# Order of the work inside the turns of the middle stage of a two-layer graph kernel

## The chip, the cores and the metric

The kernel runs on one core of one Trainium2 chip. The metric is the device time of one execution in microseconds (us). Beside the plain executions there is one profiled execution, and every row below is from its trace. Engines are named as in the profile: PE is TensorE, PEld its weight loads, DVE is VectorE, ACT is ScalarE, POOL is GpSimd, SP is SyncE.

## What is computed

100,000 nodes with 32 features and 50,000 edges, sorted by destination. Two residual layers:

```python
h = relu(layernorm(x))
m = einsum('ek,ei,kio->eo', basis(edge_attr_2), h[src], weight)       # 9 basis functions
x = x + segment_sum(m, dst) / max(degree, 1) + h @ root_w.T + root_b  # layer 1
h = relu(layernorm(x))
g = gat_conv(h)                    # 8 heads, softmax over a node's edges and itself
g = layernorm(g + h) * g1 + be1
g = relu(g @ w1 + b1) @ w2 + b2 + g
x = x + layernorm(g) * g2 + be2    # layer 2
```

For most nodes no edge ends there, and their second layer needs only their own row. They are all computed as if this held. The rows of nodes with edges are computed a second time in edge order and written over the first ones at the end.

## The kernel before

**Tiles.** A tile is 125 partitions by 16 rows of 32 features (125x512). The edges are 25 chunks of such a tile (5 blocks of 5, `NB`, `NJ`), the nodes 50 units. A product of a tile first transposes it (four PE transpositions into a bank of `T`, `transpose`, L490; ACT copies the bank into `xT` or `hT`), then multiplies it into a bank of `C` (`product`, L499). There are two `T` banks and two `C` banks, each used in turn, so the third use of a kind waits until the first one's reader is done (`t_done`, `c_done`).

**Stages.** The first stage (to about 710 us) does layer 1's norm and messages. The middle stage, `b_turn` on four engines (PE L652, ACT L968, DVE L1439, SP L342), does three node steps and four edge steps. A later stage (`d_turn`, then `x_early`) gathers the sources' rows of layer 1 for the attention; the last one scatters the finished rows. POOL issues all indirect DMAs of 125 rows each: 400 gathers by source in the first stage, then 400 gathers by destination and 400 scatters of layer 1's rows in the middle stage (for each chunk: `scatter_x1` of chunk c, L448, then `gather_dst` of chunk c+5, L443), 400 gathers in the stage after (they start when all scatters have landed, L467), and 400 scatters at the end (L478).

**Turns.** A chunk takes two turns of the middle stage, a block ten, and the whole stage 50 and two more. `turn(h)` (L108) says which steps a turn holds:

- the unit's steps, in three turns one after the other: `n1` (transpose the node rows, centre them: `product` with `center`; DVE makes relu rows in `hrow` 1), `n2` (transpose those, product with `base_bd` and a bias; DVE divides by the deviation, `hrow` 2), `n3` (transpose those, ACT applies g1 and be1, four products `hidden` (L529), ACT relu, then `back_product` (L536): a bias, 4 centring and 16 small products into one `C` bank, and `finish_rows` (L1401) on DVE, whose `unit_done` lets SP store the unit).
- the edges' steps: `e1` (transpose the gathered rows, centre) in even turns, `e2` (transpose the relu rows, product with `root_bd`) in odd ones; DVE then adds the carried and scaled message sums, which `aggregate` (L1430) makes ready with five operations, and `x1_ready` (L1466) lets POOL scatter the chunk and PE begin `e3`; `e3` (transpose, centre, relu rows) in the next even turn and `e4` (product with `base_bd` through a `T` bank in `to_T`, L550, and the attention logits through a `C` bank, `logits_dst`, L1411) in the next odd turn.

In a block units start in turns 0, 1, 3, 4, 6, 7 and 9 (L48). So n3 and n2 stand in turns 2, 5, 8, n3 and n1 in 3, 6, 9, n2 and n1 in 0, 4, 7, and all three in turn 1.

Every centring product is followed by the same norm chain: ACT squares the bank (`square`, L917), DVE sums it (`spread`, L1231), ACT takes the root (`root`, L925), DVE inverts it (L1240) and scales the rows (`relu_rows`, L1247, or `rows_over_std`, L1254), which also frees the bank. All engines work through their own list in order, so the order in `b_turn` is written out by hand four times.

Of the kernel before, what the change touches and what calls it, by code (L numbers as in the profile page):

```python
# [52 lines left out]
CREDIT = 4  # L53
# [62 lines left out]
def gnn_program(nc, x, src, dst, edge_attr, w0, root_w, root_b, w_gat, att_src, att_dst, bias_gat,  # L116
# [10 lines left out]
    with ExitStack() as ctx:  # L127
# [357 lines left out]
        def _(pe):  # L485
# [4 lines left out]
            def transpose(rows, then=None):  # L490

                at, bank = tq.next()
                pe.wait_ge(t_done, tq.room)
                for g in range(G):
                    i = nc.tensor.transpose(T[bank][:, g * P:(g + 1) * P], rows[:, g * GF:(g + 1) * GF], ident[0:P, 0:P])  # L495
                    i.then_inc(t_ready, 1) if g == G - 1 else None
                return at
# [31 lines left out]
            def hidden(nT, quarters=range(4)):  # L529

                for t in quarters:
                    at, bank = fq.next()
                    pe.wait_ge(f_done, fq.room)
                    mm(V[4 - fq.depth + bank][:, 0:WT], w1_q[:, t, :], nT, start=True, stop=True).then_inc(f_ready, 1)  # L534

            def back_product(nT):  # L536

                at, bank = cq.next()
                pe.wait_ge(c_done, cq.room)
                mm(C[bank][0:P, :], ones[:, 0:P], bias_row[:, 1, :], start=True, stop=True, skip_group_check=True)  # L540
                for g in range(G):
                    mm(C[bank][0:P, g * GF:(g + 1) * GF], nT[:, g * P:(g + 1) * P], center[:, :], start=False, stop=True, skip_group_check=True)  # L542
                for t in range(4):
                    pe.wait_ge(f_done, fq.at - 3 + t + 1 + CREDIT)
                    for g in range(G):
                        i = mm(C[bank][0:P, (4 * g + t) * F:(4 * g + t + 1) * F], hid[:, t, g * P:(g + 1) * P], w2_c[:, :],  # L546
                               start=False, stop=True, skip_group_check=True)
                i.then_inc(c_ready, 1)
# [103 lines left out]
            def b_turn(b, at):  # L652
                t = {}
                if "n3" in at:
                    pe.wait_ge(c_done, st["n2"] + 1 + CREDIT)
                    t["n3"] = transpose(unit(hrow, 2))
                if "n2" in at:
                    pe.wait_ge(c_done, st["n1"] + 1 + CREDIT)
                    t["n2"] = transpose(unit(hrow, 1))
                if "n3" in at:  # L660
                    pe.wait_ge(t_done, t["n3"] + 1 + CREDIT)
                    hidden(xT[:, 2, :])
                if "e3" in at:
                    j, back = at["e3"]
                    pe.wait_ge(x1_ready, (b - back) * NJ + j + 1)
                    t["e3"] = transpose(unit(rows_out, j))
                if "e4" in at:
                    pe.wait_ge(c_done, st["e3"] + 1 + CREDIT)
                    t["e4"] = transpose(normed(4))
                if "n2" in at:  # L670
                    st["n2"] = product(hT[:, 1, :], base_bd[:, :], bias=0, t_at=t["n2"])
                if "e1" in at:
                    j = at["e1"][0]
                    pe.wait_ge(ring_dma[j], (NB + b + 1) * DMAS)
                    t["e1"] = transpose(unit(ring, j))
                if "e2" in at:
                    pe.wait_ge(c_done, st["e1"] + 1 + CREDIT)
                    t["e2"] = transpose(unit(hrow, 0))
                if "n1" in at:
                    k = at["n1"][0]  # L680
                    pe.wait_ge(unit_in[k], (b + 1) * 16)
                    t["n1"] = transpose(place(k))
                if "e3" in at:
                    st["e3"] = product(hT[:, 2, :], center[:, :], t_at=t["e3"])
                if "e4" in at:
                    to_T(hT[:, 3, :], base_bd[:, :], bias=0, t_at=t["e4"])
                    product(hT[:, 3, :], att_bd[:, :, :].rearrange("f t h -> f (t h)"), n=8 * H)
                if "n3" in at:
                    back_product(xT[:, 2, :])
                if "e1" in at:  # L690
                    st["e1"] = product(xT[:, 0, :], center[:, :], t_at=t["e1"])
                if "e2" in at:
                    product(hT[:, 0, :], root_bd[:, :], plus=ring[0:P + 1, at["e2"][0], :], t_at=t["e2"], frees=ring_used)
                if "n1" in at:
                    st["n1"] = product(xT[:, 1, :], center[:, :], t_at=t["n1"])


            pe.wait_ge(v_done, 12 * NC + CREDIT)
# [207 lines left out]
        def _(act):  # L906
# [5 lines left out]
            def evac(to, rows=128, width=WT, func=ACT.Copy, **kw):  # L912
                at, bank = tq.next()
                act.wait_ge(t_ready, at + 1)
                nc.scalar.activation(to, T[bank][0:rows, 0:width], func, **kw).then_inc(t_done, 1)  # L915
# [52 lines left out]
            def b_turn(b, at):  # L968
                if "n3" in at: affine()
                if "n2" in at: evac(hT[:, 1, :])  # L970
                if "e3" in at: evac(hT[:, 2, :])
                if "e4" in at: evac(hT[:, 3, :])
                if "n3" in at: hidden()
                if "n2" in at: square(2)
                if "e1" in at: evac(xT[:, 0, :])
                if "e2" in at: evac(hT[:, 0, :])
                if "n2" in at: root(2)
                if "n1" in at: evac(xT[:, 1, :])
                if "e3" in at: square(4); root(4)
                if "e4" in at:  # L980
                    j, before = at["e4"]
                    k, saves = j % 2, 3 - j % 2
                    if isinstance(b, int) and b - before == 0:
                        if j > 1: act.wait_ge(base_saved[k], 16 * (j // 2))
                    else:
                        act.wait_ge(base_saved[k], 16 * ((b - before) * saves + j // 2))
                    evac(unit(base_out, k), rows=P, width=W)
                    act.wait_ge(t_done, tq.at + 1 + CREDIT)
                    act.sem_inc(base_ready, 1)
                    cq.next()  # L990
                if "n3" in at: square(3)
                if "e1" in at: square(0)
                if "e2" in at: cq.next()
                if "n3" in at: root(3)
                if "e1" in at: root(0)
                if "n1" in at: square(1); root(1)
            tq.restart(); cq.restart(); fq.restart()
            for h in range(HALVES):
                b_turn(0, turn(h, first=True))
# [139 lines left out]
        def _(dve):  # L1139
# [297 lines left out]
                step(v.tensor_tensor(slots(rows), slots(rows), wide(degree[0:P, here]), ALU.mult))  # L1437

            def b_turn(b, at):  # L1439
                norm = {}  # L1440
                if "n2" in at: norm["n2"] = spread(2)
                if "e3" in at: norm["e3"] = spread(4)
                if "e2" in at: aggregate(b, b * NJ + at["e2"][0])
                if "n2" in at: rows_over_std(2, norm["n2"])
                if "e3" in at:
                    j, back = at["e3"]
                    relu_rows(4, norm["e3"])
                    dve.wait_ge(c_done, cq.at + 1 + CREDIT)
                    v.tensor_scalar(diff[0:P, bass.ds(((b - back) * NJ + j) * W, W)], normed(4), 0.0, None, ALU.max)
                if "e4" in at:  # L1450
                    j, back = at["e4"]
                    logits_dst((b - back) * NJ + j)
                if "n3" in at: norm["n3"] = spread(3)
                if "e1" in at: norm["e1"] = spread(0)
                if "n3" in at:
                    rows = place(at["n3"][0])
                    finish_rows(rows, rows, norm["n3"], unit_done)
                if "e1" in at: relu_rows(0, norm["e1"])
                if "e2" in at:
                    j, c = at["e2"][0], b * NJ + at["e2"][0]  # L1460
                    if not isinstance(b, int) or b > 0:
                        dve.wait_ge(rows_landed[j], b * DMAS)
                        dve.wait_ge(x1_saved[j], 16 * b)
                    _, rows = bank_ready()
                    v.tensor_tensor(unit(rows_out, j), rows, msgs[0:P, bass.ds(c * W, W)], ALU.add).then_inc(c_done, 1)
                    v.tensor_copy(index_out[0:P, j, :], scatter_to[0:P, bass.ds(c * CE, CE)]).then_inc(x1_ready, 1)  # L1466
                if "n1" in at: relu_rows(1, spread(1))
            cq.restart()
            steps.restart()
            for h in range(HALVES):  # L1470
# [312 lines left out]
```

## Time and profile before

| | us |
|---|---|
| median of 3 executions | 3253.76 |
| lowest, highest | 3248.36, 3260.42 |
| the profiled execution, its own time | 3263.96 |
| its span from the first to the last instruction | 3262.2 |
| mean granted TensorE clock, share of full speed | 0.794 |

The profile gives start and length of each instruction, and for an engine's idle time the instruction that ended it. "issue" means that nothing the profile shows was waited for.

### The profile page before, as it was taken

To read this page: it belongs to the slowest core of one execution; us is meant where nothing else is said; L and a number is where in the kernel's file an instruction comes from. 1 tells how busy PE (TensorE), PEld (TensorE's weight loads), DVE (VectorE), ACT (ScalarE), POOL (GpSimd) and SP (SyncE) were. 2 spreads that over 40 slices of the span, in tenths; PEclk is the share of its full clock that TensorE was granted. 3 is DMA by queue.
4 is the path that set the end of the run, shared out by engine and by line. 5 is a ranking of instruction groups with operands and counts; after the bars stand their busy time and mean duration, and the time that the engine had idled before them with its cause. 6 is when DMAs were issued, how large, how long until landed. Compare 5 with 4: busy or idle time off the path is not lost.

```text
span 3262.2 us, 33511 instructions
## 1 busy us (share of the span) xinstructions
PE 2247.2 (69%) x10666; PEld 1570.5 (48%) x10666; DVE 1858.0 (57%) x3253; ACT 839.7 (26%) x1614; POOL 2458.8 (75%) x2011
## 2 busy tenths in 40 slices
PE   2787777747777777777777645747767547888740
PEld 1555555525555655565565534534444334454420
DVE  4889889983433433334334322346767567898720
ACT  1333233213322223223222222322222222222210
POOL 7778777887878878787787488888783075878877
PEclk9989889977888778777777766767888667888775
DMA  2333233221111112212111111111110110111100
GB/s 59 85 72 78 68 76 79 53 57 28 38 37 33 39 39 41 40 32 43 37 36 30 24 13 31 25 18 28 21 24 9 45 16 16 40 28 28 35 10 10
DMA packets 116212, 123.93 MB, mean 38 GB/s; under 512 B 70726, under 2 KB 72747, under 8 KB 116070
## 3 DMA queue, kind: packets, MB, share of 16 engines
q0 software_dynamic: 64000, 30.57, 10.0%
q1 hardware_dynamic: 52070, 91.52, 8.8%
q8 instruction: 82, 1.34, 0.2%
q14 instruction: 60, 0.49, 0.0%
HBM read 59.51 MB, written 64.00 MB: 38 GB/s over the span
## 4 chain that ended last, share of the span: by engine, by line
PE 35%; DVE 23%; POOL 22%; issue 11%; ACT 6%; SPq 2%; DMA 1%; DVEq 0%; ACTq 0%; POOLq 0%
POOL ring L430 15%; PE C L546 7%; PE V L534 7%; POOL out_rows L478 6%; PE C L510 5%; PE T L495 3%; DVE region L1595 3%; PE V L795 3%; DVE var L1235 3%; PE C L540 2%; PE C L542 2%; ACT sq L923 2%; DVE region L1587 2%; DVE region L1338 2%; ACT hid L934 2%
## 5 line engine op out<-in xcount | busy, mean ns | idle before, releaser
L430 POOL DMA_INDIRECT ring<-in_x,index x800 | 979.3, 1224 | 244.4 <-issue 243.2
L478 POOL DMA_INDIRECT out_rows<-ring,index_out x400 | 496.7, 1242 | 278.3 <-DVE ring L1407 158.9
L1235 DVE TENSOR_REDUCE var<-sq 125x16 f32<-125x512 f32 x325 | 220.7, 681 | 791.9 <-ACT sq L923 791.4
L452 POOL DMA_INDIRECT x_table<-region,index_out x400 | 483.3, 1208 | 152.4 <-issue 121.0
L430 POOL DMA_INDIRECT ring<-x_table,index x400 | 496.5, 1241 | 124.5 <-issue 123.9
L534 PE MATMUL V<-xT,w_q 128*128 128x500 f32 x600 | 369.0, 766 | 74.2 <-ACT hid L934 41.0
L923 ACT ACTIVATE sq<-C 125x512 f32<-125x512 f32 x300 | 179.4, 598 | 903.5 <-PE C L546 527.0
L510 PE MATMUL C<-center,xT 128*125 128x128 f32 x1400 | 246.2, 335 | 104.9 <-DVE hrow L1257 70.0
L546 PEld LDWEIGHTS C<-w_c,hid 128*125 128x125 f32 x2400 | 313.5, 215 | 0.0
L546 PE MATMUL C<-w_c,hid 128*125 128x32 f32 x2400 | 312.2, 293 | 0.0
L495 PE MATMUL T<-ident,hrow 125*128 125x125 f32 x1000 | 190.1, 328 | 164.0 <-DVE hrow L1251 139.0
L510 PEld LDWEIGHTS C<-center,xT 128*125 128x125 f32 x1400 | 223.7, 240 | 146.6 <-issue 68.6
L568 PE MATMUL V<-region,hT 128*125 128x384 f32 x600 | 250.6, 532 | 61.2 <-DVE region L1330 61.2
L534 PEld LDWEIGHTS V<-xT,w_q 128*128 128x128 f32 x600 | 144.8, 257 | 259.9 <-issue 135.2
L915 ACT ACTIVATE hT<-T 128x500 f32<-128x500 f32 x250 | 146.8, 589 | 446.3 <-PE T L495 446.0
L495 PEld LDWEIGHTS T<-ident,hrow 125*128 125x128 f32 x1000 | 145.0, 173 | 207.2 <-DVE hrow L1251 119.0
L934 ACT ACTIVATE hid<-V,cols 128x500 f32<-128x500 f32 x300 | 190.5, 680 | 98.6 <-PE V L534 98.4
L1338 DVE TENSOR_REDUCE region<-region 125x128 f32<-125x1152 f32 x100 | 211.8, 2119 | 0.0
L795 PE MATMUL V<-gat_bd,hT 128*125 128x512 f32 x320 | 183.0, 694 | 27.3 <-DVE region L1587 25.2
L1595 DVE TENSOR_REDUCE region<-region 125x128 f32<-125x1024 f32 x100 | 187.9, 1899 | 0.0
L1330 DVE TENSOR_TENSOR region<-V,region 125x384 f32<-125x384 f32 x300 | 157.7, 551 | 46.0 <-PE V L568 40.2
L540 PE MATMUL C<-bias_row,ones 128*125 128x512 f32 x150 | 100.2, 756 | 92.0 <-DVE hrow L1257 91.8
(250 smaller groups left out, 3143.8 us busy)
## 6 DMA issues: line engine op xcount, KB each, us to landing
ring<-in_x,index POOLq DMA_INDIRECT x800, 3.3
nodes<-in_x SPq DMA_DIRECT2D x25, 500.0 KB
x_table<-nodes SPq DMA_DIRECT2D x25, 500.0 KB
x_plain<-nodes SPq DMA_DIRECT2D x25, 500.0 KB
nodes<-x_plain SPq DMA_DIRECT2D x50, 250.0 KB
out_rows<-nodes SPq DMA_DIRECT2D x50, 250.0 KB
x_table<-region,index_out POOLq DMA_INDIRECT x400, 2.6
ring<-x_table,index POOLq DMA_INDIRECT x400, 2.7
```

What stands on the lines that cost most here:

```text
L430: pool.indirect_dma_start(out=ring[0:P, j, s * F:(s + 1) * F], out_offset=None, in_=table, in_offset=bass.IndirectOffsetOnAxis(ap=index[0: ...
L452: pool.indirect_dma_start(out=x1_table[:, :], out_offset=bass.IndirectOffsetOnAxis(ap=index_out[0:P, j, s:s + 1], axis=0), in_=rows_out[0: ...
L478: pool.indirect_dma_start(out=out[:, :], out_offset=bass.IndirectOffsetOnAxis(ap=index_out[0:P, j, s:s + 1], axis=0), in_=ring[0:P, j, s * ...
L495: i = nc.tensor.transpose(T[bank][:, g * P:(g + 1) * P], rows[:, g * GF:(g + 1) * GF], ident[0:P, 0:P])
L510: i = mm(C[bank][0:P, g * n:(g + 1) * n], cols_T[:, g * P:(g + 1) * P], right, start=bias is None and plus is None, stop=True, skip_group_ ...
L534: mm(V[4 - fq.depth + bank][:, 0:WT], w1_q[:, t, :], nT, start=True, stop=True).then_inc(f_ready, 1)
L546: i = mm(C[bank][0:P, (4 * g + t) * F:(4 * g + t + 1) * F], hid[:, t, g * P:(g + 1) * P], w2_c[:, :], start=False, stop=True, skip_group_c ...
L795: mm(banks[bank][0:P, :], hT[:, k, g * P:(g + 1) * P], gat_bd[:, q * 512:(q + 1) * 512], start=True, stop=True).then_inc(v_ready, 1)
L934: nc.scalar.activation(hid[:, t, :], V[4 - fq.depth + bank][:, 0:WT], ACT.Relu, bias=cols[:, 0:1]).then_inc(f_done, 1)
L1235: v.tensor_reduce(unit(var, k), slots(squares(k)), AX.X, ALU.add).then_inc(var_ready, 1)
L1338: v.tensor_reduce(msgs[0:P, bass.ds(cv * W + g * GF, GF)], products[0:P, (g % 2) * KS * GF:(g % 2 + 1) * KS * GF].rearrange("p (k c) -> p ...
L1595: v.tensor_reduce(diff[0:P, c * W + g * GF:c * W + (g + 1) * GF], weighted[0:P, (g % 2) * H * GF:(g % 2 + 1) * H * GF].rearrange("p (h c) ...
```

## The change

On PE, `hidden` is split into quarters 0, 1 and 2, 3; both halves stand behind the transpositions of e3 or e4, the second one behind all transpositions. The product of n1 moves from the end of the turn to ahead of the products of e3 and e4, and `back_product` moves to the end. On ACT the same order is kept: n1's copy ahead of n2's root, the second half of `hidden` behind it, n1's square and root ahead of the edges', n3's square and root last. On DVE n2's rows and n1's rows are finished before `aggregate`, each norm is completed before the next begins, and n3's is last. No instruction is added or taken away, but each engine's list is in another order. SP and POOL keep their lists.

```diff
@@ PE
                 if "n2" in at:
                     pe.wait_ge(c_done, st["n1"] + 1 + CREDIT)
                     t["n2"] = transpose(unit(hrow, 1))
-                if "n3" in at:
-                    pe.wait_ge(t_done, t["n3"] + 1 + CREDIT)
-                    hidden(xT[:, 2, :])
                 if "e3" in at:
...
                     t["e4"] = transpose(normed(4))
+                if "n3" in at:
+                    pe.wait_ge(t_done, t["n3"] + 1 + CREDIT)
+                    hidden(xT[:, 2, :], (0, 1))
                 if "n2" in at:
                     st["n2"] = product(hT[:, 1, :], base_bd[:, :], bias=0, t_at=t["n2"])
...
                     t["n1"] = transpose(place(k))
+                if "n3" in at:
+                    hidden(xT[:, 2, :], (2, 3))
+                if "n1" in at:
+                    st["n1"] = product(xT[:, 1, :], center[:, :], t_at=t["n1"])
                 if "e3" in at:
                     st["e3"] = product(hT[:, 2, :], center[:, :], t_at=t["e3"])
                 if "e4" in at:
                     to_T(hT[:, 3, :], base_bd[:, :], bias=0, t_at=t["e4"])
                     product(hT[:, 3, :], att_bd[:, :, :].rearrange("f t h -> f (t h)"), n=8 * H)
-                if "n3" in at:
-                    back_product(xT[:, 2, :])
                 if "e1" in at:
                     st["e1"] = product(xT[:, 0, :], center[:, :], t_at=t["e1"])
                 if "e2" in at:
                     product(hT[:, 0, :], root_bd[:, :], plus=ring[0:P + 1, at["e2"][0], :], t_at=t["e2"], frees=ring_used)
-                if "n1" in at:
-                    st["n1"] = product(xT[:, 1, :], center[:, :], t_at=t["n1"])
+                if "n3" in at:
+                    back_product(xT[:, 2, :])
@@ ACT
-                if "n3" in at: hidden()
+                if "n3" in at: hidden((0, 1))
                 if "n2" in at: square(2)
                 if "e1" in at: evac(xT[:, 0, :])
                 if "e2" in at: evac(hT[:, 0, :])
+                if "n1" in at: evac(xT[:, 1, :])
                 if "n2" in at: root(2)
-                if "n1" in at: evac(xT[:, 1, :])
+                if "n3" in at: hidden((2, 3))
+                if "n1" in at: square(1); root(1)
                 if "e3" in at: square(4); root(4)
...
-                if "n3" in at: square(3)
-                if "e1" in at: square(0)
+                if "e1" in at: square(0); root(0)
                 if "e2" in at: cq.next()
-                if "n3" in at: root(3)
-                if "e1" in at: root(0)
-                if "n1" in at: square(1); root(1)
+                if "n3" in at: square(3); root(3)
@@ DVE
-                norm = {}
-                if "n2" in at: norm["n2"] = spread(2)
-                if "e3" in at: norm["e3"] = spread(4)
+                if "n2" in at: rows_over_std(2, spread(2))
+                if "n1" in at: relu_rows(1, spread(1))
                 if "e2" in at: aggregate(b, b * NJ + at["e2"][0])
-                if "n2" in at: rows_over_std(2, norm["n2"])
                 if "e3" in at:
                     j, back = at["e3"]
-                    relu_rows(4, norm["e3"])
+                    relu_rows(4, spread(4))
...
-                if "n3" in at: norm["n3"] = spread(3)
-                if "e1" in at: norm["e1"] = spread(0)
-                if "n3" in at:
-                    rows = place(at["n3"][0])
-                    finish_rows(rows, rows, norm["n3"], unit_done)
-                if "e1" in at: relu_rows(0, norm["e1"])
+                if "e1" in at: relu_rows(0, spread(0))
...
-                if "n1" in at: relu_rows(1, spread(1))
+                if "n3" in at:
+                    rows = place(at["n3"][0])
+                    finish_rows(rows, rows, spread(3), unit_done)
```

## Rows read from the trace of the kernel before

**Rows 1.** Waits of POOL from 4 to 1786 us: total us, times, longest.
```profile
POOL ring L430 <- issue: 243.2, 796, 0.7
POOL x_table L452 <- issue: 111.9, 367, 0.4
```
**Rows 2.** Timeline of POOL: start us, length us, instruction, idle before it.
```profile
735.99 1.23 POOL L452 DMA_INDIRECT x_table<-region,index_out  x1 [0.30 <-issue]
784.80 1.23 POOL L452 DMA_INDIRECT x_table<-region,index_out  x1 [0.37 <-issue]
...
1786.80 1.19 POOL L452 DMA_INDIRECT x_table<-region,index_out  x1 [2.07 <-DVE index_out L1466]
...
1839.46 1.19 POOL L452 DMA_INDIRECT x_table<-region,index_out  x1 [29.06 <-DVE index_out L1466]
...
1865.96 1.24 POOL L430 DMA_INDIRECT ring<-x_table,index  x1 [2.75 <-issue]
...
2772.89 1.19 POOL L478 DMA_INDIRECT out_rows<-ring,index_out  x1 [25.17 <-DVE ring L1407]
```
**Rows 3.** Timeline of DVE: the instruction that frees a chunk for POOL's scatters.
```profile
730.66 0.45 DVE L1466 COPY index_out<-scatter_to 125x16 int32<-125x16 int32 x1
783.68 0.16 DVE L1466 COPY index_out<-scatter_to 125x16 int32<-125x16 int32 x1
...
1190.90 0.17 DVE L1466 COPY index_out<-scatter_to 125x16 int32 x1
...
1422.98 0.16 DVE L1466 COPY index_out<-scatter_to 125x16 int32 x1
...
1838.36 0.16 DVE L1466 COPY index_out<-scatter_to 125x16 int32 x1
```
**Rows 4.** Waits of PE from 1865 to 2250 us, in the stage after.
```profile
PE T L495 <- DMA ring<-x_table,index: 63.3, 9, 11.0
PE T L495 <- issue: 26.5, 1, 26.5
```
**Rows 5.** Busy us by engine, granted clock, DMA share, GB/s in one block's window.
```profile
1190.50:1422.60 232.10, 178.38 (x860) 136.04 (x860) 89.44 (x170) 68.17 (x136) 185.78 (x153) 0.76 0.19 38
```
**Rows 6.** Waits of PE in that block, the three largest: total us, times, longest.
```profile
PE T L495 <- DVE hrow L1251: 19.2, 7, 3.1
PE C L540 <- DVE hrow L1257: 13.9, 4, 4.4
PE C L510 <- DVE hrow L1257: 7.7, 3, 2.7
```
**Rows 7.** Timeline, all engines, in turns 2 and 3 of the last block: groups of matmuls.
```profile
1657.86 3.52 PE L534 MATMUL V<-xT,w_q 128*128 128x500 f32 x8
...
1663.38 0.59 PE L495 MATMUL T<-ident,ring 125*128 125x125 f32 x4
1663.81 1.04 PE L510 MATMUL C<-center,hT 128*125 128x128 f32 x8
...
1670.83 6.77 PE L546 MATMUL C<-w_c,hid 128*125 128x32 f32 x32
...
1696.15 3.58 PE L546 MATMUL C<-w_c,hid 128*125 128x32 f32 x32
```
**Rows 8.** The same timeline: affine copy, five operations of the carried sums, first of the logits.
```profile
1681.06 0.75 ACT L915 ACTIVATE xT<-T,cols 128x500 f32<-128x500 f32 x1
...
1684.43 0.68 DVE L1434 TENSOR_TENSOR region<-carry,head 125x512 f32 x1
...
1687.61 0.69 DVE L1437 TENSOR_TENSOR region<-region,degree  x1
...
1694.65 0.29 DVE L1415 COPY region<-C 125x128 f32 x1 [6.35 <-PE C L510]
```
**Rows 9.** The same timeline: a norm chain that nothing else delays.
```profile
1699.76 0.60 ACT L923 ACTIVATE sq<-C 125x512 f32<-125x512 f32 x1 [5.42 <-PE C L546]
1700.39 0.69 DVE L1235 TENSOR_REDUCE var<-sq 125x16 f32<-125x512 f32 x1 [4.69 <-ACT sq L923]
...
1701.81 0.69 DVE L1257 TENSOR_TENSOR hrow<-C,rstd 125x512 f32<-125x512 f32 x1
...
1702.63 1.13 PE L510 MATMUL C<-center,xT 128*125 128x128 f32 x8 [1.09 <-DVE hrow L1257]
```

## The prediction

> **What bounds the kernel now.** I read the engines' waits first, POOL's before the others, because POOL is the busiest engine of the page. From 4 to 1786 us POOL waits for nobody: its idle time is 1163 pieces of 0.3 us between one indirect DMA and the next [rows 1]. It issues a scatter about every 1.49 us and a gather about every 1.52 us, so a chunk of the middle stage (16 and 16) costs it some 48 us (735.99 to 784.80 [rows 2], 48.8 with a few long ones). Its first real waits are at 1786.80 and 1839.46, for DVE's L1466, the instruction that says that a chunk of layer 1 is ready: 2.07 and 29.06 us [rows 2]. Those are chunks 23 and 24, the last two.
>
> So two things run side by side. POOL needs 48 us a chunk. The other engines' loop needs 232.1 us for a block of five, 46.4 a chunk (1190.90 to 1422.98 [rows 3]). The loop is a little faster, yet at the end it decides: its last chunk is ready at 1838.36, while POOL, which has only scatters left for the last five chunks, could have begun that scatter earlier. Without the two waits, and leaving the usual 0.3 us before each, the last scatters begin 28.8 + 1.8 = **30.5 us** earlier. The gathers of the next stage follow them (1865.96 [rows 2]).
>
> What is behind it follows these gathers. In the next stage PE waits 63.3 us in nine pieces for gathered rows, and 26.5 us for the first of them [rows 4], so an earlier start is passed on. From 2160 us on PE and DVE are the bound, started by the last of these waits, and POOL's last wait (25.17 us, until 2772.89 [rows 2]) is for DVE. After it POOL scatters without a break to the end. Nothing on this way is tied to a time of its own: what the middle stage's end gains or loses, the kernel gains or loses, one to one, but no gain above 30.5.
>
> What bounds the loop: in one block PE is busy 178.4 of 232.1 us, at a granted clock of 0.76, DVE 89.4, ACT 68.2 [rows 5]. PE is the bound with its waits: 232.1 - 178.4 = 53.7 us a block. The largest [rows 6]: 19.2 for relu rows ahead of a transposition, 13.9 for a `C` bank ahead of the back product, 7.7 for a `C` bank ahead of other products.
>
> **The change, part by part.** No instruction is added, so the parts are waits taken away and waits put in. One norm chain, from the square to the next PE instruction, takes 1702.63 - 1699.76 = 2.87 us when nothing is in its way [rows 9]; call it 2.9. On PE at full clock a transposition of a tile takes 0.43 until the next group starts (1663.38 to 1663.81 [rows 7]), a product 0.87 (1.04 less the overlap), four `hidden` 3.36, the 16 small products of a back product 3.4 and the whole of it 5.2. At the half level the small products take 6.77 instead of 3.58 [rows 7].
>
> *Removed.* n1's product was the last of a turn, and the next turn's first transposition needs its rows: the 19.2 us. Now at least one edge product and mostly the back product (5.2) stand between, more than 2.9, and this wait goes to zero in the turns with n3. n2's bank was needed by the back product just two products later; on DVE n2's scaling stood even behind the five operations of `aggregate` (1684.43 to 1688.30 [rows 8], 3.9 us). Now n2's norm is first on DVE: the 13.9 and most of the 7.7 go too. Together 38 to 41 us a block.
>
> *Added, at the head of a turn.* ACT's last work is square and root of n3, behind the back product. The root is over 1.7 us after the product's end, the affine copy takes 0.75 more [rows 8], and the third transposition needs the bank that it frees. PE can do only two transpositions (0.9) meanwhile: a wait of 1.85 us in 7 turns a block. In turns 5 and 1 the copy stands behind e1's root instead, 2.4 to 2.9.
>
> *Added, ahead of the back product.* In turns 2 and 8 it needs e3's bank, with only e1's product (0.87) in between: 2.9 - 0.87 = 2.1 us. In turn 6 e1 waits for n1's bank (2.2), the back product for e3's, where DVE takes one chain after the other (1.2). In turns 3, 9 and 1 it needs the logits' bank, and on DVE the logits stand behind `aggregate`, which now stands behind n1's rows. Counting turn 3 from its start: n1's product ends at 7.9, its rows are done at 10.7, `aggregate` at 14.7, the logits at 15.4. PE comes to the back product at 12.6: 2.9 us. (Before, `aggregate` ran while DVE was idle, 6.35 us ahead of the logits [rows 8].) In turn 5 the same costs 1.3.
>
> *Added, elsewhere.* In turn 8 the transposition of e3 now comes ahead of `hidden` and waits for x1 of turn 7, 3.1 us. In turns 0 and 4, n1, e3, e1 have two banks among them and no long work to hide a chain: 1.2 + 0.5 + 1.6, and 1.65 at the head, 5.0.
>
> I wrote each turn out in this way, at full clock:
>
> | turn | 0 | 1 | 2 | 3 | 4 | 5 | 6 | 7 | 8 | 9 | block |
> |---|---|---|---|---|---|---|---|---|---|---|---|
> | PE's waits, us | 5.0 | 5.7 | 4.0 | 5.1 | 5.0 | 3.6 | 5.2 | 3.2 | 5.3 | 5.1 | 47 |
>
> *The sum.* 53.7 - 47 = 6.7 us a block is the least, because PE's groups at the half level take up to twice as long and cover more of the 2.9 us chains. PE's own work at full clock is some 127 us a block by the lengths above; it is busy 178, so about 40% of the work runs at the half level. If that share of the new waits is covered, they are 28 to 40, and the gain is 14 to 25 us. From chunk 0 to chunk 24 there are 4.8 blocks: 32 us with the least, up to 120. Add that in a turn x1 now comes ahead of the back product and not behind it, some 2 us. So chunk 24 is ready 34 us earlier or more, and POOL's 30.5 are gone in full, with little to spare at the low end. The remaining PE gain is hidden: POOL issues without a break from 4 us to the end of the scatters, and that is the new bound. As a check of the first chunks: chunk 0 must be ready before POOL's 735.99. It is ready at 730.66; n1's rows ahead of `aggregate` make that about 2.5 us later, still in time. Chunk 1 had 0.9 us to spare (783.68 against 784.80 [rows 2, 3]); it will come 10 us or more earlier.
>
> SP: a unit's store now waits longer in its turn (finish rows is last), and behind it in SP's queue are the x1 store and the next index load. The unit and index loads have eight turns and one turn of POOL's lag; I take it at nothing, and at worst it costs POOL a wait of a few us. POOL's list is the same, so nothing moves there.
>
> The profiled execution took 3263.96, so 3233.5 with the change. It lies 10.2 above the median. If that lies in the stages behind, the median becomes 3223.3; if the loop's end was that much later in it, POOL's floor stands and the median becomes 3233.5. Nearer to the first: **3226**.
>
> **The rivals.** *The loop gains, but less than POOL's wait.* Each of the hand-worked waits may be longer by the 0.1 us steps between engines; 2 us a block less and worse cover give 10 to 28 us. Time 3226 to 3244. The least of the sum, 32, is close to the 30.5, which speaks for it; chance 0.17.
>
> *New waits outweigh (slower).* The place is `aggregate` between n1's rows and the logits, in the four turns with e4 and a back product. I count 10 us there a block. It decides once ACT's and DVE's fixed orders add more than 6.7 us over my 47: for example 3 us more in each of these turns and 0.5 in the rest is 15 a block, net 8, and over 4.8 blocks chunk 24 comes 40 us later: 3294. For it: DVE and ACT now stop at each norm for the root instead of doing the next sum. Against: DVE is busy only 89 of 232 us. Chance 0.07.
>
> *The clock falls.* Granted 0.76 in the block [rows 5], on both levels, 1.2 and 2.4 GHz. If half of PE's work instead of 40% runs at the lower level, PE is busy 190 instead of 178, and the gain of 6.7 becomes a loss of 6 a block: 29 us, 3283. A sentence of the Trainium skill speaks for this (TensorE: Matmul & The Clock Gate, "A second HAM failure mode: psum-queue depth-cycling"): going round PSUM banks with short idle pieces between the groups makes the clock swing, and the change splits one group and puts short waits between the rest. By that rule alone one would forecast slower. The rows speak against it: the longest waits (4.4 and 3.1 [rows 6]) go, and the same work is packed tighter. Chance 0.06.
>
> *No effect.* The early start of the gathers is lost behind, to the DVE and PE chain or to another clock there, or half of it: 3240 to 3256. The 63.3 us of waits for gathered rows [rows 4] speak against it. Chance 0.10.
>
> *Forecast as worked out:* 0.60, with 3212 to 3237.
>
> **How the numbers follow.** About 0.5% (16 us) is what a measurement of this kernel can tell from no change. Faster by more than that, under 3237.5: 0.60 and a third of the first rival, 0.66. Within it: two thirds of that rival, most of "no effect", a little of the slower ones, 0.22. Slower: 0.12. The range 3210 to 3258 takes the forecast, the partial gain and no effect, and leaves the slower cases out.
>
> **What would show it.** POOL without waits over 1 us up to the gathers of the next stage, which start at about 1835; L1466 of chunk 24 before 1808; a block's period under 226 and the waits on L1251 ahead of transpositions near zero in turns with n3; new waits of PE for ACT's affine copy (about 2 us, 7 a block) and for the logits' bank. A wait of POOL for L1466 that stays, or a longer block, makes the prediction wrong; so do gathers that start 30 us earlier with an end that doesn't.

## The result and the profile after

| us | before | changed |
|---|---|---|
| median | 3260.42 (13 executions) | 3236.48 (13 executions) |
| lowest, highest | 3241.42, 3276.47 | 3233.78, 3242.16 |
| profiled execution, its span | 3263.96, 3262.2 | 3233.78, 3231.9 |
| mean granted clock | 0.794 | 0.809 |

The ratio is 0.992, with a 95% interval of 0.9903 to 0.9938: some 26 us faster (24 by the two medians), and clear of noise. The profiled executions differ by 30.2 us.

The timeline of POOL in the changed kernel answers to [rows 2]:

```profile
736.44 1.23 POOL L452 DMA_INDIRECT x_table<-region,index_out  x1 [1.33 <-issue]
...
1838.10 1.23 POOL L430 DMA_INDIRECT ring<-x_table,index  x1 [2.75 <-issue]
...
2742.67 1.19 POOL L478 DMA_INDIRECT out_rows<-ring,index_out  x1 [25.17 <-DVE ring L1408]
```

The two waits for a chunk of layer 1 (2.07 and 29.06 us before) are gone. The gathers of the next stage start at 1838.10 instead of 1865.96, 27.9 us earlier, and POOL's last wait, the same 25.17 us long, ends 30.2 us earlier. POOL's three largest entries in the list of waits of the changed kernel:

```profile
POOL ring L430 <- issue: 368.1, 1198, 2.8
POOL out_rows L478 <- DVE ring L1408: 158.3, 9, 116.0
POOL x_table L452 <- issue: 122.9, 400, 1.3
```

Up to the last stage there is only the time between two DMAs ("issue"). The page's chain of work that ended last says the same. Before, it went through PE for 35% of the span and POOL for 22%. Now:

```profile
POOL 53%; issue 16%; PE 15%; DVE 14%; ACT 2%; DMA 1%; POOLq 0%; DVEq 0%; ACTq 0%
```

So the place that the change worked on is off the chain. The instruction that frees a chunk, L1460 now, in DVE's timeline (chunks 0 and 24; [rows 3] before):

```profile
735.27 0.16 DVE L1460 COPY index_out<-scatter_to 125x16 int32<-125x16 int32 x1
...
1746.39 0.17 DVE L1460 COPY index_out<-scatter_to 125x16 int32 x1
```

The last chunk is ready at 1746.39 and not at 1838.36: the loop gained 92 us, three times what the kernel did. The windows of three blocks, from chunk 2 to 7, from 7 to 12 and from 14 to 19, first of the kernel before and then of the changed one (busy us of PE, PEld, DVE, ACT and POOL, then granted clock, DMA share, GB/s):

```profile
828.85:1054.25 225.40, 166.82 (x862) 127.11 (x861) 89.25 (x170) 68.15 (x136) 180.44 (x148) 0.82 0.19 37
1054.25:1286.60 232.35, 178.66 (x861) 136.09 (x861) 89.10 (x171) 68.16 (x136) 186.02 (x153) 0.76 0.19 37
1374.15:1606.27 232.12, 176.83 (x860) 134.71 (x860) 89.46 (x170) 68.17 (x136) 185.54 (x153) 0.77 0.20 38
```

```profile
805.89:991.07 185.18, 147.33 (x861) 110.92 (x860) 91.16 (x171) 69.58 (x136) 148.45 (x121) 0.92 0.21 42
991.07:1185.45 194.38, 158.49 (x861) 118.33 (x860) 90.62 (x171) 70.26 (x136) 155.53 (x128) 0.85 0.21 42
1261.83:1500.83 239.00, 165.26 (x861) 125.24 (x860) 90.30 (x170) 71.14 (x136) 191.14 (x158) 0.80 0.19 37
```

The first block takes 185.2 us where it took 225.4. PE's idle time in it fell from 58.6 to 37.9 us, and its busy time for the same 860 matmuls from 166.8 to 147.3, at a granted clock of 0.92 instead of 0.82. The second block takes 194.4 where it took 232.4: 17.8 us less of idle time and 20.2 less of busy time, at 0.85 instead of 0.76. The third window of the changed kernel is slower than the loop can go. Between 730 and 1800 us PE has a wait that was not there before, for the gathered rows, and it is now the largest:

```profile
PE T L495 <- DMA ring<-in_x,index: 85.1, 10, 13.6
```

The loop uses up the gathered chunks that are in store at its beginning, and then runs at POOL's pace: POOL's first scatters of chunk 0 and of chunk 20 start at 736.44 and 1715.05, 48.9 us a chunk or 245 a block.

### The profile page after: what moved, and what is told of

It is laid out like the page before. It is cut to its first block, busy times and chain, and to the rows that moved or that the text cites. A ratio compares the mean times of both kernels' runs of the same rounds, so it can differ in the third digit from the quotient of the medians.

```text
span 3231.9 us, 33522 instructions
## 1 busy us (share of the span) xinstructions
PE 2165.0 (67%) x10666; PEld 1499.7 (46%) x10666; DVE 1864.0 (58%) x3253; ACT 851.6 (26%) x1614; POOL 2459.2 (76%) x2011
## 4 chain that ended last, share of the span: by engine, by line
POOL 53%; issue 16%; PE 15%; DVE 14%; ACT 2%; DMA 1%; POOLq 0%; DVEq 0%; ACTq 0%
POOL ring L430 33%; POOL x_table L452 14%; POOL out_rows L478 6%; DVE region L1591 3%; PE V L797 3%; PE C L546 3%; PE V L534 2%; DVE region L1583 2%; PE C L510 1%; PE T L495 1%; DVE region L1267 1%; PE C L540 1%; PE C L542 1%; DVE var L1236 1%; DVE region L1339 1%
## 5 line engine op out<-in xcount | busy, mean ns | idle before, releaser
L478 POOL DMA_INDIRECT out_rows<-ring,index_out x400 | 496.4, 1241 | 277.4 <-DVE ring L1408 158.3
L925 ACT ACTIVATE sq<-C 125x512 f32<-125x512 f32 x300 | 178.7, 596 | 852.8 <-PE C L546 538.7
L510 PE MATMUL C<-center,xT 128*125 128x128 f32 x1400 | 224.8, 313 | 96.6 <-DVE hrow L1252 37.1
L546 PEld LDWEIGHTS C<-w_c,hid 128*125 128x125 f32 x2400 | 282.0, 197 | 0.0
L546 PE MATMUL C<-w_c,hid 128*125 128x32 f32 x2400 | 281.9, 277 | 0.0
L510 PEld LDWEIGHTS C<-center,xT 128*125 128x125 f32 x1400 | 205.1, 220 | 150.7 <-issue 64.2
L495 PE MATMUL T<-ident,ring 125*128 125x125 f32 x300 | 61.6, 342 | 304.4 <-DMA ring<-in_x,index 154.7
L534 PEld LDWEIGHTS V<-xT,w_q 128*128 128x128 f32 x600 | 134.1, 244 | 224.8 <-issue 103.4
L1241 DVE RECIPROCAL rstd<-std 125x16 f32<-125x16 f32 x350 | 87.3, 249 | 233.7 <-ACT std L930 232.8
L495 PE MATMUL T<-ident,hrow 125*128 125x125 f32 x1000 | 177.9, 316 | 65.6 <-DVE hrow L1252 36.8
L495 PEld LDWEIGHTS T<-ident,ring 125*128 125x128 f32 x300 | 43.9, 177 | 329.6 <-issue 172.3
L917 ACT ACTIVATE xT<-T 128x500 f32<-128x500 f32 x175 | 101.5, 585 | 359.1 <-PE T L495 357.6
```

The source lines that it names most:

```text
L478: pool.indirect_dma_start(out=out[:, :], out_offset=bass.IndirectOffsetOnAxis(ap=index_out[0:P, j, s:s + 1], axis=0), in_=ring[0:P, j, s * ...
L510: i = mm(C[bank][0:P, g * n:(g + 1) * n], cols_T[:, g * P:(g + 1) * P], right, start=bias is None and plus is None, stop=True, skip_group_ ...
```

## The experiments

Two questions: is POOL's issue really what cuts the gain off, and which parts of the change speed the loop up? Each kernel was timed beside the kernel before. "Free period" is the time from chunk 2 to chunk 7; up to chunk 12 PE has no wait for gathered rows in any of these profiles, so the block from chunk 7 to 12 is free too, and the table below has both. The periods are from one profiled execution each.

### Less work for POOL: half_before, half_after

In both kernels 8 of the 16 scatters of each chunk are left out in the middle stage, so half of layer 1's rows for edges don't reach the table. The waits are counted to match.

```diff
                 pool.sem_inc(cleared, 1)
-                for s in range(CE):
+                for s in range(CE // 2):
                     pool.indirect_dma_start(
                         out=x1_table[:, :],
...
-            pool.wait_ge(rows_landed[j], NB * DMAS)
+            pool.wait_ge(rows_landed[j], NB * DMAS // 2)
```

> The kernel before, with 8 of the 16 scatters of each chunk in the middle stage left out (POOL has 36 us of work a chunk instead of 48; half the rows of layer 1 don't reach the table). Theory 1 (the loop of PE, DVE and ACT bounds the middle stage before the change, POOL is only just behind): chunk 24 is ready at the same time, about 1838 us, and only the last scatter is 12 us shorter: 12 us faster than the kernel before, some 3248. Rival (POOL's pace already slows the loop in the kernel before): 100 us faster or more.

> The changed kernel, with the same 8 of 16 scatters of each chunk left out. Theory 1 (the change took some 43 us from each block of the loop, and POOL's issue hides all but 30 of it): the loop runs at its own pace of 185 to 190 us a block to the end, chunk 24 is ready at about 1640 to 1660, the next stage's gathers start at about 1660, and the time is 3050 to 3070, some 190 below half_before. Rival (the fast pace is only possible while the gathered rows are in store, or the loop gained only the 30 us that show): 3190 to 3225, 25 to 60 below half_before.

Measured: half_before 3246.63 us, a ratio of 0.9961 (0.9939 to 0.9983), 13 us faster, as the shorter last scatter has it. The forecast of the time held. That of chunk 24 (ready at about 1838) did not in the profiled execution, the fastest of ten: it is ready at 1819.02, the later blocks taking 222 us each. In this profile it is POOL that waits in the middle stage, for layer 1:

```profile
POOL x_table L452 <- DVE index_out L1466: 309.5, 20, 41.0
```

half_after 3069.67 us, 0.9404 (0.9375 to 0.9433): 177 us below half_before. In the profile its last chunk is ready at 1645.61, and chunks 14 to 19 take 194.6 us. So the loop before was its own bound, and the changed loop is faster by 38 us in the first block (187.7 against 225.4), by 27 in the last (194.6 against 221.8 of half_before), and by 173 at chunk 24. The change is worth 177 us where POOL has some 36 us of work a chunk, and 26 where it has 49. The forecast for half_after held, at its upper edge; of the rival there (60 us at most) nothing is left.

### More work for PE: pad4, pad12

```diff
-                mm(C[bank][0:P, :], ones[:, 0:P], bias_row[:, 1, :], start=True, stop=True, skip_group_check=True)
+                for _ in range(1 + again):
+                    mm(C[bank][0:P, :], ones[:, 0:P], bias_row[:, 1, :], start=True, stop=True, skip_group_check=True)
```

This is in `back_product`, with `again` 4 or 12 in the middle stage alone.

> The changed kernel with four more copies of the bias matmul ahead of each back product (same values; some 0.85 us each, so 3.4 us a unit, 24 us a block). Theory 1 (the loop has about 50 us a block in hand under POOL's 241): no change, 3236, chunk 24 ready later than 1746 but before 1808. Rival (the gain of the change stands close to the edge, as the prediction's 6.7 to 25 us a block had it): chunk 24 comes after 1808 and the time is 3250 to 3320.

> The changed kernel with twelve more copies of the bias matmul ahead of each back product (10.2 us a unit, 71 us a block). Theory 1: the loop needs 188 + 71 less what the added work hides of waits, some 240 to 255 a block, about POOL's 241 or over it: between no change and 80 us slower, 3236 to 3320. Rival (waits of the loop hide most of the added work): no change. If the loop had gained only what shows, the time would be over 3500.

pad4: 3239.31 us, 0.9919 (0.9888 to 0.9949), the changed kernel's time, with a free period of 215.9 us and the last chunk at 1769.79. 31 us more in this block, and 24 in the next, cost nothing, as expected. pad12: 3417.61 us, 1.0465 (1.0433 to 1.0498), 98 us over the top of what I expected. Its window of chunks 14 to 19:

```profile
1459.18:1725.34 266.16, 229.55 (x1029) 148.14 (x1028) 91.13 (x170) 70.24 (x136) 194.66 (x161) 0.90 0.18 34
```

A block takes 266.2 us, the 194.6 of half_after and all the 71 added. PE still waits 37 us a block: the waits hid none of the added work, where I had let them hide 4 to 19. The last chunk is ready at 1991.61, 153.3 us later than in the kernel before, and the profiled span is 3418.9, 156.7 us more: what the end of the middle stage loses is passed on one to one. The edge lies between pad4's 218 us a block and pad12's 266, and POOL's 245 lie in that gap; I had put them at 241.

### One part taken back: agg_first, hid_whole, back_mid, n1_only

`agg_first` has the sums of the edge rows first on DVE:

```diff
+                if "e2" in at: aggregate(b, b * NJ + at["e2"][0])
                 if "n2" in at: rows_over_std(2, spread(2))
                 if "n1" in at: relu_rows(1, spread(1))
-                if "e2" in at: aggregate(b, b * NJ + at["e2"][0])
```

> The changed kernel with aggregate first in DVE's turn, ahead of n2's and n1's rows. Theory (the wait of the back product for the logits' bank comes from aggregate standing behind n1's rows): that wait, 41 us over the middle stage, goes; the free block period falls from 185 to 190 us to about 175 to 183; total time unchanged, 3236, since POOL is the bound. Rival (n2's and n1's rows come later and cost as much): period the same or longer, total the same.

`hid_whole` has `hidden` in one piece ahead of the transposition of e3 or e4:

```diff
+                if "n3" in at:
+                    pe.wait_ge(t_done, t["n3"] + 1 + CREDIT)
+                    hidden(xT[:, 2, :])
                 if "e3" in at:
...
-                    hidden(xT[:, 2, :], (0, 1))
...
-                    hidden(xT[:, 2, :], (2, 3))
```

> The changed kernel with the four hidden matmuls whole again and ahead of the transpositions of e3 and e4, on PE and ACT. Theory (the gain is from the order of n1 and the back product, not from the split): free period 188 to 200 us a block, total 3236. Rival (the split keeps PE fed and its clock up): period 210 or more, then chunk 24 comes near 1808 and the total is 3236 to 3260.

`back_mid` has the back product, and with it n3's norm on ACT and DVE, ahead of the last edge product:

```diff
+                if "n3" in at:
+                    back_product(xT[:, 2, :])
                 if "e1" in at:
                     st["e1"] = product(xT[:, 0, :], center[:, :], t_at=t["e1"])
...
-                if "n3" in at:
-                    back_product(xT[:, 2, :])
```

> The changed kernel with the back product (and n3's norm on ACT and DVE) ahead of e1's and e2's products again. Theory (the back product at the end hides n1's and e1's norm chains): the transposition of e2 waits again for e1's rows, ahead of it only one product: free period 200 to 220 us, total 3236. Rival (n1 ahead is what counts, the back product's place nothing): period as in the changed kernel, 185 to 190.

`n1_only` takes back both of these edits together.

> The changed kernel with both the whole hidden group and the back product in their old places, so that what is left of the change is n1's product and norm ahead of the edges' and DVE's new order. Theory (each part gives its own share: the split hidden some 27 us a block, the back product's place nothing): free period 208 to 218 us a block, total 3236 +- 4. Rival (back product last pays only where hidden is whole, and both go together): period 225 or more, total 3240 to 3262.

And the reverse, `before_agg_late`: the kernel before with one edit of DVE's order.

```diff
-                if "e2" in at: aggregate(b, b * NJ + at["e2"][0])
                 if "n2" in at: rows_over_std(2, norm["n2"])
+                if "e2" in at: aggregate(b, b * NJ + at["e2"][0])
```

> The kernel before with one part of the change: on DVE n2's rows ahead of aggregate. Theory (the back product waited for n2's bank behind aggregate, 13.9 us a block in four pieces, two of them lengthened by 2 us or more): period falls from 232 by 5 to 8 us and chunk 24 comes 25 us earlier or more, total 3235 to 3245. Rival (a shorter wait there is only moved to the next one): period 232, total as before, 3260.

All times, and two blocks of each profile. In the two columns of blocks stand the period, PE's busy and its idle time in it, and the granted clock:

| kernel | median us | ratio (interval) | chunks 2 to 7 | chunks 7 to 12 | last chunk ready |
|---|---|---|---|---|---|
| before | 3260 | | 225.4: 166.8, 58.6, 0.82 | 232.4: 178.7, 53.7, 0.76 | 1838.4 |
| before_agg_late | 3236.57 | 0.9916 (0.9900 to 0.9933) | 211.5: 164.8, 46.7, 0.81 | 204.8: 157.5, 47.4, 0.84 | 1760.0 |
| hid_whole | 3234.11 | 0.9919 (0.9902 to 0.9936) | 212.0: 162.8, 49.2, 0.85 | 215.0: 166.2, 48.9, 0.83 | 1753.2 |
| n1_only | 3238.97 | 0.9935 (0.9913 to 0.9957) | 199.4: 152.3, 47.1, 0.88 | 201.5: 155.4, 46.0, 0.86 | 1759.0 |
| back_mid | 3239.18 | 0.9928 (0.9912 to 0.9945) | 187.6: 150.1, 37.5, 0.89 | 187.9: 150.6, 37.3, 0.88 | 1756.6 |
| changed | 3236.48 | 0.9920 (0.9903 to 0.9938) | 185.2: 147.3, 37.9, 0.92 | 194.4: 158.5, 35.9, 0.85 | 1746.4 |
| agg_first | 3235.38 | 0.9919 (0.9902 to 0.9935) | 180.8: 153.5, 27.3, 0.87 | 183.3: 154.8, 28.5, 0.86 | 1742.8 |

The windows of chunks 7 to 12 behind two of these rows, before_agg_late and then back_mid:

```profile
1032.53:1237.34 204.81, 157.46 (x861) 119.19 (x860) 89.30 (x170) 68.08 (x136) 163.97 (x135) 0.84 0.20 41
```

```profile
999.27:1187.18 187.91, 150.59 (x860) 115.27 (x860) 89.97 (x171) 70.83 (x136) 150.80 (x122) 0.88 0.22 44
```

What follows (the first block is that of chunks 2 to 7, the second that of 7 to 12):

- Every version has the same total within its interval, whatever its loop does between 181 and 218 us a block. That is the cut-off again, in six versions and pad4.
- One moved line in the kernel before gives the whole of what shows: `before_agg_late`. It takes 14 us off the first block and 27.5 off the second, against the 5 to 8 expected. Of the 27.5 only 6.3 are idle time; the other 21.2 are the same matmuls at a granted clock of 0.84 instead of 0.76. (In half_before, whose loop is that of the kernel before, the later blocks took 222 us at 0.82, so part of this may be the execution and not the line.)
- `aggregate` behind n1's rows costs 4 us in the first block and 11 in the second, and 10.6 and 7.4 of PE's idle time; what I expected of agg_first held (175 to 183 for the first block). The first block of agg_first has the least idle time but a lower clock than the changed kernel's (0.87 against 0.92), so the clock doesn't follow the idle time alone.
- Halving `hidden` gives 26.8 and 20.6 us where the back product is last (hid_whole), and 11.8 and 13.5 where it is not (n1_only against back_mid). In each case less than that is idle time (11.3 and 13.0, 9.6 and 8.7); the rest is PE's busy time at a higher clock. The expected 188 to 200 for hid_whole was too fast.
- With the split group the place of the back product is worth nothing that these rows show: at the end it gains 2.4 us in the first block and loses 6.5 in the second. Without the split, the end costs 12.6 and 13.6 (hid_whole against n1_only). My expectation for back_mid (200 to 220) was wrong, and so was n1_only's (208 to 218).
- So of the 30.9 us that n1_only takes off the second block, DVE's one line alone takes 27.5 (14 of 26.0 in the first). That line is the largest part, the split the next, and n1's product with the rest of the new order adds 3.4 to 12.1.

### Where POOL isn't the bound: half_agg_first

The changed kernel with the edits of half_after and agg_first together.

> half_after (8 of 16 scatters left out in the middle stage, changed kernel) with aggregate first on DVE. Where POOL is not the bound, the loop's period should show one to one: 194.6 a block falls to about 181, 4.8 blocks, so 50 to 70 us below half_after's 3070: 3000 to 3020, if POOL's 36.3 a chunk (181 a block) leaves it that much. Rival (the free period of 181 in agg_first holds only at the beginning): within 20 us of half_after.

3003.66 us, 0.9218 (0.9196 to 0.9239): 66 us below half_after. That is what I expected (3000 to 3020). The blocks take 177 to 187 us, and chunk 24 is ready 60 us earlier. This gain of the loop shows in full once POOL has less to do, and the order with `aggregate` first is the better one of the two, though nothing shows of it in the real kernel. POOL waits for layer 1 only four times here (65.3 us in all), so it is close to being the bound again.

### The same order in the stage behind: d_order

The turns of the next stage have the same unit steps. The edit, on PE (ACT and DVE in the same order):

```diff
+                if "n1" in at:
+                    st["n1"] = product(xT[:, 1, :], center[:, :], t_at=t["n1"])
                 if not last:
                     st["d1"] = product(xT[:, 0, :], center[:, :], t_at=t["d1"], frees=ring_used)
                 if "n3" in at:
                     back_product(xT[:, 2, :])
-                if "n1" in at:
-                    st["n1"] = product(xT[:, 1, :], center[:, :], t_at=t["n1"])
```

> The changed kernel with the same order in the turns of the stage after: n1's product, norm and copy ahead of the edge product's, the back product and n3's norm last, on PE, ACT and DVE. Theory (that stage is paced by POOL's gathers to 2130 us and by PE's chain of waits from there on, with 8 units left; a wait for relu rows of some 2.5 us goes at each): 5 to 20 us faster than the changed kernel, 3217 to 3231. Rival (x_early's products lie between these turns and hide the chains already, and the new head-of-turn wait takes as much): within 4 us of 3236.

3229.59 us (3225.17 to 3230.56, 5 executions), a ratio to the kernel before of 0.9898 (0.9880 to 0.9915). The changed kernel's 13 executions lie at 3233.78 and above, so this beats both, by some 7 us more, at the small end of the 5 to 20 that I expected. (The two ratios were taken at different times, and their intervals overlap; the executions don't.) In its profile POOL's waits for finished rows are:

```profile
POOL out_rows L478 <- DVE ring L1405: 151.4, 6, 110.1
```

That is 6.9 us less than in the changed kernel (158.3), although its gathers start 1.8 us later (1839.86). The last wait ends 3.4 us earlier (2739.27 against 2742.67), in the slowest of its five executions against the fastest of the changed kernel's thirteen. This stretch is on the chain, so here a shorter wait shows.

## Why the prediction was right

The predicted 3226 us (3210 to 3258, faster) stands against 3236.48. For the profiled execution the working gave 3233.5, and it took 3233.78.

- **The ceiling of 30.5 us: right, and it made the number.** 27.9 us at the start of the gathers. Of the rest, 0.5 us is chunk 0: it was ready at 735.27, 4.6 us later than before and not 2.5, POOL waited 1.33 instead of 0.30 for it, and its first scatter starts at 736.44 instead of 735.99. The other 2 us are POOL's own: from the first scatter of chunk 0 to that of chunk 20 it took 978.6 us instead of 976.1, for which no row shows a reason. These rows also put POOL at 48.8 us a chunk before, not at the 48 that I reckoned with.
- **One to one behind it: right.** 27.9 became 30.3 at the end, and in pad12 153.3 became 156.7.
- **Which of two medians: the higher.** I left open whether the 10.2 us by which the profiled execution lay above the median of three stood in the loop's end or behind it, and leaned to the lower time. With 13 executions the median before is 3260.42, and the changed kernel lies at its floor with a spread of 8 us where it had 35.
- **The waits taken away: right.** PE's waits for L1251 ahead of transpositions are no longer in its list. In the kernel before, in the block from chunk 2:

```profile
PE T L495 <- DVE hrow L1251: 22.2, 7, 3.6
```

- **The waits put in: mostly right.** The largest in the changed kernel's block (chunks 2 to 7):

```profile
PE C L540 <- DVE region L1418: 8.6, 4, 2.7
PE C L510 <- DVE hrow L1252: 5.2, 3, 2.0
PE T L495 <- ACT xT L917: 5.1, 3, 2.2
PE C L540 <- DVE region L1252: 4.0, 3, 1.8
PE V L534 <- ACT xT L917: 3.7, 3, 1.5
...
PE T L495 <- DVE index_out L1460: 2.5, 1, 2.5
```

  The logits' bank has its four pieces with 8.6 us (10 worked out), the affine copy 8.8 in six pieces (13 in seven; 3.7 of it is ahead of `hidden`, where 5.0 stood before), the back product for e3's bank up to 1.8 (2.1), the transposition of e3 for x1 once, 2.5 (3.1). In all 37.9 us against 47 at full clock and 28 to 40 with cover. The sum took its 47 as all of PE's waits, though it had named only 38 to 41 of the old 53.7 as taken away, and gave no reason for the other 13; the total came out right even so.
- **The step that failed: the sum of the loop, "the gain is 14 to 25 us" a block with 6.7 as the least.** It was 40.2 (225.4 to 185.2), and 38.0 in the next block (232.4 to 194.4). The part of it that is idle time, 20.7 and 17.8, lies inside my 14 to 25. What I left out is PE's busy time, which I kept as it was: it fell by 19.5 and 20.2 us, as the granted clock rose from 0.82 to 0.92 and from 0.76 to 0.85. (My 127 us of work at full clock look low as well: busy time times clock, an estimate, is 135.6 in the block of [rows 5], and 136.8 and 135.5 in the blocks from chunk 2 before and after.) That chunk 24 came 92 us earlier, inside my 34 to 120, is luck: the loop alone gained 173 (half_before to half_after), and waiting for the gathers that POOL issues (85.1 us) took the rest back. So the remark that 30.5 us are reached "with little to spare at the low end" was wrong too: chunk 24 comes 62 us before the 1808 that were needed, and pad4 shows that 24 to 31 us more a block can be spent. The number was saved by the ceiling, which hides an error of that size.
- **SP's part, taken at nothing: right.** Between 730 and 1800 us neither PE nor POOL waits for one of SP's transfers.
- **Gathers as the loop's second bound: left out.** From about chunk 12 PE waits for them, 85.1 us in all. It changed nothing in the total, since POOL issues these gathers and is the bound of both.
- **The rivals.** "Less than POOL's wait" and "new waits outweigh" fall with the 92 us of the loop and with POOL's two waits gone; the median alone could not tell the first of them from the forecast, since 3236.48 lies in the range of both. "The clock falls" had the wrong sign: the clock rose. The section "A second HAM failure mode: psum-queue depth-cycling" of TensorE: Matmul & The Clock Gate, in the Trainium skill, names micro-idles between groups as what makes the clock swing. In the block from chunk 2 PE's idle time came in 28 pieces of 2.1 us on average and up to 4.4, and comes now in 27 of 1.4 us and up to 2.7, and the granted clock rose. So the trace does not bear out my reading that the new order would make the clock worse: the pieces got shorter, and not more. That fewer or shorter idle pieces are what raised it is not shown: agg_first has less idle time at a lower clock, and no run changes the idle pieces alone.

## What to carry to other kernels

When two engines run side by side at nearly the same pace, work out the second one's pace before you price a gain on the first: here a gain of 173 us in the loop became 92 and then 26, because POOL needed 48.8 us a chunk and the loop 46.4. In a loop with short dependent chains look first at what stands ahead of the norm that the next product needs, and at groups that can be split; and count the clock: about half of what the loop gained was not waiting at all, but the same matmuls at a higher granted clock. And try the smallest piece first; one moved line gave all that could show.

## What was not expected of the hardware

- The same 860 matmuls of a block kept PE busy for 176.8 us at a granted clock of 0.77, 166.8 at 0.82 and 147.3 at 0.92, with no more change to the kernel than the order of its work. What raises the clock stays open.
- PE's idle time hid none of the work added ahead of the back product: with 71 us of matmuls added a block the period grew by 71.6 (194.6 in half_after to 266.2), and the idle time stayed at 37.
- Executions of the kernel before lie between 3241 and 3276 us, of the changed one between 3234 and 3242. A stage that is bounded by POOL's even issue instead of the loop fits this, but pad12, which the loop bounds, has a spread of only 5 us (3415.81 to 3420.66). What makes the kernel before waver stays open; its loop has different periods within one execution already (225.4 and 232.4).
